# A post-norm decoder layer on one core: earlier first projections, two waits moved, another order of all steps

## The chip, the cores and the metric

The kernel runs on one core of one Trainium2 chip. The metric is device time in microseconds (us), the median of three runs; smaller is better. Inside the core, TensorE (PE) multiplies matrices, VectorE (DVE) and ScalarE (ACT) work on the results in PSUM and SBUF, GpSimd (POOL) does a few masks and sums, and DMAs are issued from the queues of SyncE (SP), ACT and POOL.

## What is computed

One transformer layer over x and ctx of shape (16, 128, 128), float32: self-attention with relative positions, causal cross-attention with ctx, and a feed-forward part with eight routed experts and a shared one. After each of the three, the residual is added and the sum normalised.

```python
# self-attention: E = 128, H = 16 heads of 8, relative positions clipped at 20
attn = softmax((q @ k.T + q @ rk2.T) / sqrt(8))
x = layernorm(x + ((attn @ v + attn @ rv2) @ Wo.T + bo))
# cross-attention, causal: queries from x, keys and values from ctx
x = layernorm(x + softmax(mask(cq @ ck.T / sqrt(8))) @ cv @ cWo.T + cbo)
# feed-forward: probs = softmax(x @ router_w + router_b), the best 2 of 8 experts, one shared expert
x = layernorm(x + gelu(x @ sw1 + sb1) @ sw2 + sb2
                + sum_e weight_e * (gelu(x @ rw1[e] + rb1[e]) @ rw2[e] + rb2[e]))
```

## The kernel before

The 16 sequences are worked in four chunks of four (512 tokens). All work of a chunk is cut into named steps, and one string, `SCHEDULE` (lines 74 to 102), lists the steps of all chunks in one order: the digit ahead is the chunk, a number behind a dot the tile. Every engine's program, and SP's queue, walks this same list (`for s in ORDER`) and executes its own part of each step. Inside an engine nothing overtakes, so a step that waits holds back all that stands behind it on that engine. The string is written out by hand or by a planner outside the kernel; no time is worked out at run time.

The steps of a chunk, in the order of their data:

- `load`, `loadc`: SP loads x (four DMAs, L340) and ctx (one DMA, L345). Chunk 0's are issued ahead of the list, `load` of chunk 1 at its place in it. A load of x for chunk 2 or later waits for the residual sum of two chunks before.
- `xT`: PE transposes x (L515), ACT copies it (L761). `q`, `k`, `v`: the projections (PE L520 for q and k, L526 for v). Each of q, k, ck and cq is split into three bf16 parts: ACT writes the high part (L789), DVE the rest (L922), ACT the middle (L791), DVE the low part (L926). Then SP writes the parts to DRAM (`parts_by_head<-part`, L389) and, in the step `st_q`, `st_k`, `st_ck` or `st_cq`, waits for that write and reads them back stacked by head into QS or KS with three DMAs (L404). `v` and `cv` end in a DVE add of the value bias (L933).
- `bias` (8 tiles, PE L636, ACT copy L799): relative-position scores. It needs stacked q.
- `p1` (8 tiles, PE L547): scores, which DVE adds (L943) and reduces to maxima (L946). It needs stacked k. `m` (twice): PE transposes the maxima, DVE splits them in three (L958 to L969), ACT and SP send them into rows of QS (L775, L412). `p2` (8 tiles, PE L556) takes the maxima off; DVE adds (L974), ACT takes the exponential (L803).
- `pv`, `w2`, `pvT`, `w2T` (4 each): values, relative values and transposes back. `X`, `XT`, `o`, `ln`: divide, project, add the residual, normalise. `x1T`, `cq` start the cross-attention.
- `cT`, `ck`, `cv`; `c1` (8 tiles, maxima by DVE L950), `cm`, `c2` (8 tiles, exponential L810), `cpv`, `cpvT`, `cX`, `cXT`, `co`, `cln`: cross-attention, which needs `st_ck` and `st_cq`.
- `x2T`, `r`, `g`, `up` (18 matmul steps, PE L714, GELU on ACT L846), `dn` (9, PE L725, DVE L1060), `fln` (last normalisation on DVE, L886 to L896, and the store of the output from SP, L432).
- `wts`: the weights of cross-attention are transposed (PE L507). `lrv`: relative values by way of DRAM. `lex`: ten DMAs on SP (L371 to L384) load all expert weights and biases.

PE has two large PSUM slots for `bias`, `p1`, `p2`, `c1`, `c2` and four small ones for the rest; each use waits until the slot's last user has been read.

Around the change: PE executes `wts` and `xT` first and, behind the first `xT`, the transposes of the self-attention weights and of the bias columns (L598). Then `q`, `k` and `v` of chunk 0 wait (L609 and L610) for `wt_sb` to reach 3. ACT counts `wt_sb` up once for the weights of q and k (L744), once for those of v and o (L746) and once for the bias columns (L766). The fourth use of a small slot waits in addition for a DVE memset of that bank (L878). DVE waits at L879 for all four value and output biases before it begins the list. The first `ADD` that reads them is the one of `v`.

Of the kernel before, what the change touches and what calls it, by code (L numbers as in the profile page):

```python
# [80 lines left out]
0cpv.1 0c2.5 0c2.6 1m.1 2q 0c2.7 2st_q 1pv.0 0cpv.2 0cpvT.0 1p2.2 0cpvT.1 1p2.3 1pvT.0 1p2.4 0cpv.3 0cpvT.2  # L81
1p2.5 1pv.1 1p2.6 0cpvT.3 1p2.7 0cX 1cv 1pv.2 1ck 1w2.0 0cXT 2k 1pvT.1 1w2.1 1w2.2 1pv.3 0co 1w2.3 1pvT.2 1pvT.3
2bias.0 2bias.1 0cln 1st_ck 1w2T.0 1w2T.1 1w2T.2 2bias.2 1w2T.3 0x2T 2bias.3 1X 2bias.4 0r 1XT 2v 2bias.5 0up.0
1o 2bias.6 0up.1 0g 1ln 2bias.7 0up.2 2p1.0 0dn.0 1x1T 2st_k 2p1.1 2cT 1cq 0up.3 2p1.2 2p1.3 0up.4 1st_cq 0up.5
0dn.1 0up.6 3load 0up.7 2p1.4 2p1.5 0up.8 0dn.2 1c1.0 0up.9 0up.10 2m.0 3xT 1c1.1 1c1.2 0dn.3 1c1.3 1c1.4 0up.11
1c1.5 1cm.0 0up.12 0up.13 2p2.0 0dn.4 2p2.1 1c1.6 0dn.5 1c2.0 1c2.1 0dn.6 1c1.7 1c2.2 2ck 1cpv.0 1c2.3 2pv.0
2p2.2 1cm.1 1cpvT.0 0up.14 2p1.6 0up.15 0up.16 0up.17 2p2.3 2p1.7 1cpv.1 0dn.7 1c2.4 1c2.5 2m.1 3q 0dn.8 1c2.6
1c2.7 1cpv.2 2pv.1 2p2.4 2pvT.0 1cpvT.1 2p2.5 1cpvT.2 2p2.6 1cpv.3 2p2.7 2cv 2pvT.1 2pv.2 1cpvT.3 2w2.0 2pvT.2
# [1010 lines left out]
```

## Time and profile before

| | us |
|---|---|
| median of three runs | 451.35 (451.09 to 451.75) |
| profiled execution | 451.89 |
| its span, first to last instruction | 450.1 |
| PE busy in the span | 378.3 |
| DVE busy | 303.4 |
| ACT busy | 228.3 |
| POOL busy | 80.0 |

The profile is of one execution, on which the trace gives each instruction's start and duration. PE busy counts matmuls with modelled ends. "issue" names time in which an engine waited for nothing that the profile shows. A row of SPq, ACTq or POOLq is the issuing of DMAs, not their transfer.

### The profile page before, as it was taken

Reading aid. Unit: us, or ns where it says so; the run is one execution under the profiler, and the core shown is the slowest. Engines: PE = TensorE matmul, PEld = TensorE weight load, DVE = VectorE, ACT = ScalarE, POOL = GpSimd, SP = SyncE. Lnnn points to the kernel's source line nnn. Section 1 sums busy time; section 2 is a strip of 40 time slices with the busy share of each in tenths; the row PEclk is TensorE's granted clock in tenths of the full one; section 3 lists DMA queues with packets and bytes.
Section 4 is the critical chain, followed back from the end, with each engine's and each line's share of the span. In section 5 each row is a group of like instructions: output and inputs, shape, how many; then the busy total and the mean of one; then the engine's idle time right before and its main releaser. Section 6 shows DMA issues by size and latency. Waiting matters only on the chain.

```text
span 450.1 us, 11284 instructions
## 1 busy us (share of the span) xinstructions
PE 378.3 (84%) x4714; PEld 285.1 (63%) x4729; DVE 303.4 (67%) x630; ACT 228.3 (51%) x329; POOL 80.0 (18%) x92
## 2 busy tenths in 40 slices
...
GB/s 93 73 183 39 4 51 248 202 71 128 28 4 41 108 178 1 128 4 4 39 39 82 214 4 106 4 37 4 75 3 2 100 31 6 1 1 0 25 1 23
DMA packets 29420, 26.87 MB, mean 60 GB/s; under 512 B 12673, under 2 KB 27962, under 8 KB 28602
## 3 DMA queue, kind: packets, MB, share of 16 engines
...
q8 instruction: 38, 0.62, 0.6%
q10 hardware_dynamic: 3136, 0.27, 0.5%
q14 instruction: 12, 0.10, 0.1%
q0 software_dynamic: 192, 0.03, 0.0%
...
## 4 chain that ended last, share of the span: by engine, by line
PE 54%; DVE 17%; DMA 10%; issue 6%; ACT 5%; SPq 5%; POOL 1%; POOLq 0%; DVEq 0%; ACTq 0%
PE ps_f L725 9%; PE ps_s L547 9%; PE ps_f L714 8%; PE ps_f L573 6%; PE ps_f L581 4%; DMA parts_by_head<-part 3%; PE ps_f L677 3%; PE ps_f L520 3%; DMA QS<-parts_by_head 3%; DVE ST L943 3%; PE ps_s L540 3%; DVE MX L946 3%; PE ps_s L556 2%; PE ps_f L526 2%; PE ps_s L636 2%
## 5 line engine op out<-in xcount | busy, mean ns | idle before, releaser
L547 PE MATMUL ps_s<-QS,KS 125*128 125x128 bf16 (+1 forms) x768 | 79.5, 249 | 11.9 <-DVE ST L943 6.6
L547 PEld LDWEIGHTS ps_s<-QS,KS 125*128 125x128 bf16 (+1 forms) x768 | 65.1, 106 | 34.6 <-DVE ST L943 9.0
L846 ACT ACTIVATE HT<-ps_f,hb 128x512 f32<-128x512 f32 x72 | 48.3, 688 | 74.0 <-PE ps_f L714 44.3
L725 PEld LDWEIGHTS ps_f<-w,HT 128*128 128x128 f32 x576 | 68.8, 192 | 8.1 <-issue 6.0
L725 PE MATMUL ps_f<-w,HT 128*128 128x128 f32 x576 | 72.1, 276 | 0.1
L714 PE MATMUL ps_f<-x2T,w 128*128 128x512 f32 x144 | 70.8, 602 | 1.4 <-DVE acc L1056 1.0
L488 POOL TENSOR_SCALAR_AFFINE_SELECT PC<-PC 128x1024 f32<-128x1024 f32 x32 | 34.8, 1094 | 142.2 <-ACT PC L810 142.2
L1060 DVE SCALAR_TENSOR_TENSOR acc<-ps_f,gw,acc 128x128 f32<-128x128 f32 x128 | 35.7, 341 | 21.8 <-PE ps_f L725 21.5
L810 ACT ACTIVATE PC<-ps_s 128x1024 f32<-128x1024 f32 x32 | 32.2, 1024 | 33.4 <-PE ps_s L547 30.1
L803 ACT ACTIVATE ST<-ST 128x1024 f32<-128x1024 f32 x32 | 33.9, 1061 | 28.0 <-DVE ST L974 27.6
L943 DVE TENSOR_TENSOR ST<-ps_s,ST 128x1024 f32<-128x1024 f32 x32 | 38.6, 1207 | 11.0 <-PE ps_s L547 10.9
L974 DVE TENSOR_TENSOR ST<-ps_s,ST 128x1024 f32<-128x1024 f32 x32 | 38.2, 1216 | 8.6 <-PE ps_s L556 8.2
L950 DVE TRANSPOSE_TENSOR_REDUCE MX<-ps_s 128x32 f32<-128x1024 f32 x32 | 38.7, 1232 | 3.8 <-PE ps_s L547 3.6
L946 DVE TRANSPOSE_TENSOR_REDUCE MX<-ST 128x32 f32<-128x1024 f32 x32 | 39.8, 1245 | 1.1
L494 POOL TENSOR_TENSOR ve<-mv,epst 128x4 f32<-128x4 f32 x12 | 2.4, 202 | 197.1 <-DVE mv L890 197.1
L714 PEld LDWEIGHTS ps_f<-x2T,w 128*128 128x128 f32 x144 | 24.1, 191 | 16.3 <-issue 13.9
L799 ACT COPY ST<-ps_s 128x1024 f32<-128x1024 f32 x32 | 30.9, 1025 | 6.9 <-PE ps_s L636 6.9
L540 PE MATMUL ps_s<-maskT,identb 128*128 128x512 bf16 x64 | 25.8, 402 | 8.7 <-DMA QS<-parts_by_head 5.8
L922 DVE SCALAR_TENSOR_TENSOR rest<-ps_f,bcol,part 128x512 f32<-128x512 f32 x16 | 11.9, 743 | 22.0 <-ACT part L789 22.0
L636 PE MATMUL ps_s<-QS,RK 125*128 125x64 bf16 x512 | 20.5, 197 | 5.9 <-issue 3.7
L636 PEld LDWEIGHTS ps_s<-QS,RK 125*128 125x128 bf16 x512 | 18.9, 101 | 7.9 <-issue 4.4
L556 PE MATMUL ps_s<-QS,onesr 128*128 128x512 bf16 x49 | 17.4, 422 | 6.9 <-DMA QS<-MP 4.3
...
## 6 DMA issues: line engine op xcount, KB each, us to landing
...
QS<-MP SPq DMA_DIRECT2D x32, 8.0 KB, 2.1
```

Source lines behind the costliest of these rows:

```text
L488: nc.gpsimd.affine_select(out=w, in_=w, compare_op=ALU.is_ge, fill=0.0, base=0, pattern=[[0, HB_TILE], [1, S]], channel_multiplier=-1).the ...
L540: nc.tensor.matmul(ps[:, half * BANK:(half + 1) * BANK], identb[:, :], maskT[:, :, :].broadcast_to([P, 4, S]), start=True, stop=False, ski ...
L547: last = nc.tensor.matmul(ps[:, o:o + S], KS[a][0:kd, c:c + S], queries(a, kd, h, j), start=not masked and j == 0, stop=j == NB - 1, skip_ ...
L636: last = nc.tensor.matmul(ps[:, j * HB:(j + 1) * HB], RK[0:KZ, S - 1 - q:2 * S - 1 - q], qs_q[:, :, q, :], start=True, stop=True)
L714: nc.tensor.matmul(ps[:, :], w1[:, e, f * P:(f + 1) * P], x2T[:, :], start=True, stop=True).then_inc(f_full, 1)
L725: last = nc.tensor.matmul(ps[:, b * E:(b + 1) * E], HT[n % 2][:, f, b * S:(b + 1) * S], w2[:, e, f, :], start=f == 0, stop=f == NF - 1 and ...
L846: nc.scalar.activation(HT[n % 2][:, f, :], ps[:, :], ACT.Gelu, bias=hb[:, e, f:f + 1]).then_inc(ht_ready, 1)
L943: nc.vector.tensor_tensor(by_bank(w), ps[:, :].rearrange("p (c b q) -> p c q b", b=2, q=S), by_bank(w), ALU.add).then_inc(sum_ready, 1)
L946: nc.vector.tensor_reduce(MX[0][:, t * 32:(t + 1) * 32], w.rearrange("p c (g i) -> p c g i", i=QD), AXIS.X, ALU.max, apply_transpose=True) ...
L950: nc.vector.tensor_reduce(MX[1][:, t * 32:(t + 1) * 32], ps[:, :].rearrange("p (c i) -> p c i", i=QD), AXIS.X, ALU.max, apply_transpose=Tr ...
L974: nc.vector.tensor_tensor(w, ps[:, :].rearrange("p (c i) -> p c i", i=ST_PAIR), w, ALU.add).then_inc(sc_ready, 1)
L1060: last = nc.vector.scalar_tensor_tensor(acc[:, b, :], ps[:, b * E:(b + 1) * E], gw[ch % 2][:, b, t - 1:t], acc[:, b, :], ALU.mult, ALU.add)
```

## The change

Three edits. `q` and `k` of chunk 0 wait for the first weight copy alone, `v` for the second. DVE's wait for the value biases moves from ahead of the list to the first `v` and the first `cv`. And `SCHEDULE` is replaced by another order of the same steps.

```diff
                     if ch == 0:
-                        pe.wait_ge(wt_sb, 3)
+                        pe.wait_ge(wt_sb, 2 if what == "v" else 1)
...
             nc.vector.memset(ps_f[3][:, :], 0.0).then_inc(c_dve, 1)
-            v.wait_ge(ld_br, 16 * 4)
...
                     if ch:
                         done_f(v, (ch - 1, "cpv" if a else "pv", NQ - 1))
+                    else:
+                        v.wait_ge(ld_br, 16 * 4)
```

The order, cut to its head and to the places of which the prediction speaks:

```diff
-0xT 1xT 0load 1load 0loadc 0q 0st_q 0k 0v 0st_k 0wts 0cT 0ck 0cv 0bias.0 0bias.1 0bias.2 0bias.3 0bias.4 0bias.5
-0bias.6 0bias.7 0p1.0 0p1.1 0p1.2 0p1.3 0p1.4 0m.0 0p1.5 0lrv 0p1.6 0p2.0 0p1.7 0p2.1 0m.1 0p2.2 0pv.0 0p2.3
-0p2.4 0lex 0pvT.0 0p2.5 0pv.1 0p2.6 0p2.7 1q 1st_q 0pv.2 0w2.0 0w2.1 0pvT.1 0pvT.2 0st_ck 0pv.3 1k 0w2.2 0w2.3
-1v 0pvT.3 0w2T.0 0w2T.1 0w2T.2 0w2T.3 1bias.0 1bias.1 0XT 1bias.2 1loadc 0X 1bias.3 0o 1bias.4 0ln 1st_k 1bias.5
-1bias.6 1bias.7 1p1.0 0x1T 1cT 0cq 1p1.1 1p1.2 1p1.3 1p1.4 0st_cq 2loadc 0c1.0 0c1.1 0c1.2 0c1.3 1m.0 0c1.4
-2load 0cm.0 0c1.5 0c1.6 0c1.7 1p1.5 0c2.0 0c2.1 0c2.2 0cm.1 1p2.0 1p1.6 0cpv.0 0c2.3 2xT 1p2.1 1p1.7 0c2.4
+0load 0xT 1load 0q 0k 0v 1xT 0wts 0bias.0 0bias.1 0bias.2 0bias.3 0bias.4 0st_q 0bias.5 0bias.6 0st_k 0bias.7
+0p1.0 0loadc 0p1.1 0p1.2 0p1.3 0lrv 0p1.4 0m.0 0p1.5 0cT 0p1.6 0p2.0 0p1.7 0p2.1 0m.1 0p2.2 0pv.0 0p2.3 0p2.4
+0p2.5 0pv.1 0p2.6 0pvT.0 0p2.7 1q 0pv.2 1st_q 0ck 0w2.0 0w2.1 0w2.2 0st_ck 1k 0pvT.1 1st_k 0pv.3 0w2.3 0pvT.2
+0pvT.3 0w2T.0 0w2T.1 0w2T.2 0w2T.3 1bias.0 1bias.1 0lex 0X 1v 0XT 1bias.2 1bias.3 0o 1bias.4 1bias.5 1loadc
+1bias.6 0ln 0cv 1bias.7 1p1.0 0x1T 0cq 2load 1p1.1 1p1.2 1p1.3 1p1.4 0st_cq 2xT 0c1.0 1cT 0c1.1 0c1.2 0c1.3
+0c1.4 0cm.0 0c1.5 0c1.6 0c1.7 0c2.0 0c2.1 1m.0 0c2.2 0cm.1 1p1.5 0c2.3 0cpv.0 1p2.0 1p2.1 1p1.6 0cpv.1 0c2.4
...
-3w2T.1 3w2T.2 3w2T.3 2x2T 3X 3cv 2r 3XT 2up.0 3o 1dn.8 2up.1 2up.2 2g 2up.3 3ln 1fln 3x1T 3cq 2up.4 2dn.0 2up.5
-2up.6 2dn.1 2up.7 2dn.2 2dn.3 3c1.0 3c1.1 2up.8 3st_cq 3c1.2 3c1.3 3c1.4 2up.9 3cm.0 3c1.5 2up.10 3c1.6 2up.11
-3c1.7 3c2.0 2dn.4 3c2.1 3cm.1 2dn.5 3c2.2 3c2.3 3cpv.0 3c2.4 3c2.5 3cX 3cpv.1 3c2.6 3c2.7 3cpvT.0 3cpv.2 3cpvT.1
-2up.12 3cpvT.2 3cpv.3 2up.13 3cpvT.3 2dn.6 3cXT 2up.14 3co 2up.15 3cln 2up.16 2dn.7 2up.17 3x2T 3r 3up.0 3up.1
+3pv.0 3p2.4 2cXT 3p2.5 3pv.1 3p2.6 3p2.7 2co 3pvT.0 1dn.8 2cln 3w2.0 3w2.1 1fln 3pvT.1 3pv.2 2x2T 3pv.3 2r 2up.0
+3w2.2 3w2.3 3pvT.2 3pvT.3 3w2T.0 3w2T.1 3w2T.2 3w2T.3 3X 2up.1 2g 3cv 3XT 2up.2 3o 2dn.0 2up.3 2up.4 3x1T 2up.5
+3ln 3cq 2up.6 2dn.1 2up.7 2dn.2 2up.8 2up.9 2dn.3 2dn.4 3c1.0 3c1.1 3c1.2 3c1.3 3st_cq 3c1.4 2up.10 3cm.0 3c1.5
+2up.11 3c1.6 2up.12 3c1.7 3c2.0 3c2.1 3cm.1 2dn.5 3c2.2 3c2.3 3cX 3cpv.0 3c2.4 3c2.5 3cpvT.0 3cpv.1 3c2.6 3c2.7
+3cpv.2 3cpvT.1 2up.13 3cpv.3 3cpvT.2 3cpvT.3 2dn.6 3cXT 2up.14 3co 2up.15 2up.16 3cln 2dn.7 2up.17 3x2T 3r 3up.0
...
```

## Rows read from the trace of the kernel before

**Rows 1.** Stretches: us, busy by engine, PEclk granted clock, DMA share, GB/s.

```profile
core 0: us, PE busy (x) PEld busy (x) DVE busy (x) ACT busy (x) POOL busy (x), PEclk, DMA share, GB/s
0.00:29.00 29.00, 10.48 (x46) 6.98 (x46) 13.02 (x22) 8.08 (x15) 23.04 (x30) 1.00 0.41 109
29.00:60.00 31.00, 16.63 (x198) 12.86 (x199) 21.52 (x23) 8.58 (x9) 0.00 (x0) 0.61 0.19 56
...
100.00:125.00 25.00, 14.49 (x114) 9.56 (x113) 22.70 (x29) 0.62 (x1) 0.00 (x0) 0.78 0.26 70
125.00:300.00 175.00, 172.09 (x2296) 133.59 (x2304) 142.71 (x285) 110.91 (x161) 28.42 (x30) 0.99 0.22 62
300.00:412.00 112.00, 103.60 (x1283) 76.45 (x1285) 68.51 (x182) 66.00 (x95) 23.60 (x25) 1.00 0.10 26
```

**Rows 2.** Timeline, opening, PE and DVE: start, duration, what, [idle before <- releaser].

```profile
8.06 0.27 PE L598 MATMUL ps_f<-ident,OW 4*128 4x4 f32 x1 [1.04 <-DMA OW<-in_L_xattn_bk]
...
10.46 0.48 DVE L878 MEMSET ps_f<- 128x512 f32 x1
...
14.95 1.11 PE L515 MATMUL ps_f<-ident,xin 128*128 128x128 f32 x4 [6.63 <-DMA xin<-in_x]
```

**Rows 3.** The chain that ended last, single pieces: start, duration, what.

```profile
10.41 4.50 DMA xin<-in_x
...
91.41 3.69 DMA KS<-parts_by_head
...
101.49 2.52 DMA parts_by_head<-part
...
105.22 4.26 DMA QS<-parts_by_head
...
122.53 2.00 DMA QS<-MP
...
281.93 1.84 PE ps_f L725 x16
...
292.23 1.77 PE ps_f L714 x4
```

**Rows 4.** Timeline, opening: the query parts from the high part to the first bias.

```profile
17.81 0.69 ACT L789 ACTIVATE part<-ps_f,bcol 128x512 bf16<-128x512 f32 x1 [1.06 <-PE ps_f L520]
...
20.79 0.39 SPq L389 DMA_DIRECT2D parts_by_head<-part  x1
...
23.41 1.83 SPq L404 DMA_DIRECT2D QS<-parts_by_head  x3
...
28.92 1.87 PE L636 MATMUL ps_s<-QS,RK 125*128 125x64 bf16 x32 [3.67 <-issue]
```

**Rows 5.** Timeline, opening: the key parts and the first scores.

```profile
25.29 0.58 SPq L389 DMA_DIRECT2D parts_by_head<-part  x1
...
29.89 1.74 SPq L404 DMA_DIRECT2D KS<-parts_by_head  x3
...
36.93 2.02 PE L547 MATMUL ps_s<-QS,KS 125*128 125x128 bf16 x16 [0.36 <-ACT ST L799]
```

**Rows 6.** Timeline of SP's queue, first and last expert load, chunk 1's q stack, x of chunk 2.

```profile
63.02 0.58 SPq L371 DMA_DIRECT2D rb_row<-in_L_ffn_router_b  x1
...
72.25 0.53 SPq L384 DMA_DIRECT2D wr<-in_L_ffn_router_w  x1
...
78.06 2.14 SPq L404 DMA_DIRECT2D QS<-parts_by_head  x3
...
119.47 2.08 SPq L340 DMA_DIRECT2D xin<-in_x  x4
```

**Rows 7.** Stretches again: the one in which the expert weights arrive.

```profile
66.00:76.00 10.00, 6.72 (x185) 4.19 (x185) 6.03 (x6) 8.00 (x11) 0.00 (x0) 0.98 0.86 239
```

**Rows 8.** Timeline, DVE and PE, chunk 3 ahead of its cross-attention.

```profile
350.32 2.06 DVE L896 TENSOR_SCALAR acc<-acc,mv,rstd 128x128 f32<-128x128 f32 x4 [1.40 <-POOL rstd L496]
...
363.15 0.38 PE L540 MATMUL ps_s<-maskT,identb 128*128 128x512 bf16 x1 [1.45 <-DMA QS<-parts_by_head]
```

More of the change, by code:

```diff
@@ L80 @@
-2load 0cm.0 0c1.5 0c1.6 0c1.7 1p1.5 0c2.0 0c2.1 0c2.2 0cm.1 1p2.0 1p1.6 0cpv.0 0c2.3 2xT 1p2.1 1p1.7 0c2.4
[L81 to L88, printed above, removed]
-2w2.1 3st_q 1cX 0fln 1cXT 2w2.2 3k 2pv.3 1co 3st_k 2w2.3 3bias.0 3bias.1 2pvT.3 3v 2w2T.0 3loadc 2st_ck 1cln
@@ L100 @@
-3up.2 2dn.8 3up.3 3g 3up.4 2fln 3up.5 3dn.0 3up.6 3dn.1 3dn.2 3up.7 3up.8 3up.9 3dn.3 3up.10 3up.11 3up.12 3dn.4
-3dn.5 3up.13 3up.14 3up.15 3up.16 3up.17 3dn.6 3dn.7 3dn.8 3fln
+0load 0xT 1load 0q 0k 0v 1xT 0wts 0bias.0 0bias.1 0bias.2 0bias.3 0bias.4 0st_q 0bias.5 0bias.6 0st_k 0bias.7
+0p1.0 0loadc 0p1.1 0p1.2 0p1.3 0lrv 0p1.4 0m.0 0p1.5 0cT 0p1.6 0p2.0 0p1.7 0p2.1 0m.1 0p2.2 0pv.0 0p2.3 0p2.4
+0p2.5 0pv.1 0p2.6 0pvT.0 0p2.7 1q 0pv.2 1st_q 0ck 0w2.0 0w2.1 0w2.2 0st_ck 1k 0pvT.1 1st_k 0pv.3 0w2.3 0pvT.2
@@ new lines @@
+0pvT.3 0w2T.0 0w2T.1 0w2T.2 0w2T.3 1bias.0 1bias.1 0lex 0X 1v 0XT 1bias.2 1bias.3 0o 1bias.4 1bias.5 1loadc
+1bias.6 0ln 0cv 1bias.7 1p1.0 0x1T 0cq 2load 1p1.1 1p1.2 1p1.3 1p1.4 0st_cq 2xT 0c1.0 1cT 0c1.1 0c1.2 0c1.3
+0c1.4 0cm.0 0c1.5 0c1.6 0c1.7 0c2.0 0c2.1 1m.0 0c2.2 0cm.1 1p1.5 0c2.3 0cpv.0 1p2.0 1p2.1 1p1.6 0cpv.1 0c2.4
+1p1.7 0c2.5 2q 0cpvT.0 0c2.6 0c2.7 1m.1 0cpv.2 0cpvT.1 2loadc 1pv.0 1p2.2 1p2.3 1cv 0cpv.3 1p2.4 0cpvT.2 1p2.5
+1pv.1 1p2.6 1pvT.0 1p2.7 0cpvT.3 1pv.2 0cX 1pvT.1 1ck 1w2.0 1pv.3 2st_q 2k 1pvT.2 1w2.1 2v 0cXT 1w2.2 0co 1w2.3
```

20 lines of the change are left out of this document (14 added, 6 removed).

## The prediction, written before the changed kernel ran

> **What bounds the kernel now.** I read the stretches first [rows 1]. From 125 to 300 us PE is busy 172.1 of 175.0 us, so there the time is PE's own work, and no order shortens that. Ahead of it PE lacks 18.5 us of the first 29, 14.4 of the next 31 and 10.5 of the 25 us from 100. Behind it, from 300 to 412, it lacks 8.4. The same steps are executed after the change, so the time falls by what these gaps lose, and rises by new ones. The reader should see there that a gain in the opening is kept if nothing later is tied to a fixed moment, because the saturated stretch simply starts earlier.
>
> Then the timeline of the opening [rows 2]. PE ends the bias columns at 8.33 and next works at 14.95, on the transpose of chunk 1's x, which stands ahead of 0q in the list. That x is issued last of all first loads and lands at 14.91 by the chain of waits [rows 3]. Nothing that chunk 0 needs is missing: q waits behind a step of another chunk.
>
> **The first edit** (wait for one weight copy). In PE's own order q stands behind the bias columns, whose matmul ends at 8.33 [rows 2]; the third count follows by one small ACT copy, about 0.2 us. The edit is worth 0.2 at most, and I count it within the next term.
>
> **1xT behind 0v.** q's matmuls start at 8.4. In the trace they took from 16.06 (14.95 + 1.11 [rows 2]) to the high part at 17.81 [rows 4], 1.75, so the high part starts at 10.1, ends at about 10.8, and DVE is free at 10.94, behind its memset [rows 2]. From high part to the write of the parts the trace has 20.79 - 17.81 = 2.98 [rows 4]: 13.2 with a tenth of waiting, 7.6 earlier than 20.79. The write landed in 2.62 (23.41 - 20.79, [rows 4]); k's, which shared the DMA engines with a stack, in 4.60 (29.89 - 25.29, [rows 5]). The new write shares its first 1.7 us with the end of x, so I take 3.3, nearer the first. From the stack's issue to the first bias the trace has 28.92 - 23.41 = 5.5 [rows 4]. First bias: 13.2 + 3.3 + 5.5 = 22.0, or **6.9 earlier**. With 2.62 it is 7.6; with 4.6, and 0.5 for k's write now ahead of the stack, 5.1. Below zero is excluded, since every step of that chain moves forward.
>
> Keys: k's parts are ready about 2.3 behind q's, 15.5; they land by 20.1, and st_k, behind st_q on SP, has its data by 20.1 + 1.2 + 3.7 = 25.0 (the 3.7 from [rows 3]). The eight bias tiles need 8.0 us (36.93 - 28.92, [rows 4, 5]), to 30.0. Keys are no bound, and the phase that follows, where DVE sets the pace (21.5 busy of 31 us [rows 1]), begins 6.9 earlier as a whole.
>
> **The second edit** (value biases). In the old order DVE's first piece of the list followed the high part that starts at 17.81 [rows 4], long after any bias, so the wait cost nothing. In the new order it would hold q's rest from 11.0 until the biases are there; they are issued just ahead of x, so by 14.9 at the latest [rows 3]. The edit is worth 0 to 3.9 in the new order, and is what lets the term above stand.
>
> **0cT, 0ck, 0cv out of the opening.** They hid in the wait for q's stack, so leaving it earns nothing. 0cT (about 0.6 of PE) now hides in PE's gaps of the p1 phase. 0ck comes between 1q and 0w2.0, and its write and stack stand on SP ahead of 1k's write. Queue: 1q's write as before, stack, ck's write, stack of ck, k's write, stack of k, each stack (1.8 of issuing, [rows 4, 5]) waiting for a landing of 2.5 to 4.6 [rows 3, 5]. From the issue of 1st_q to the landed keys that is 1.8 + 2.5 + 1.8 + 2.5 + 1.2 + 3.7 = 13.5, or 17.7 with both landings long, against 17.0 in the trace (91.41 + 3.69 - 78.06, [rows 3, 6]). PE reaches 1bias somewhat earlier, an estimated 1.6, as 1v moved behind its first tiles, and then waits for these keys. Ends: 1.6 gained, 0.7 lost; I take **0.3 gained**.
>
> **Expert loads (lex) later.** Before, they were issued from 63.02 to 72.78 [rows 6], and the engines were 0.86 busy at 239 GB/s from 66 to 76 [rows 7]; nobody waited. Now the same 9.8 us of issuing stand between 1st_k and the write of 0cq's parts. 1st_k ends about when 1p1.0 becomes possible less 3.7, and cq's parts are ready 10 us after it (101.49 against 91.4 [rows 3]), so the queue is free within a microsecond either way. But their transfers are still running, and x of chunk 2 (2.08 of issuing [rows 6]) now stands behind cq's write too. So I give that write 4.6, the longest of [rows 5], instead of 2.52 [rows 3]. The data of c1.0 then come 2.1 later than their 109.48; DVE has its p1 tiles in hand at that time and sets the pace there [rows 1], so I let more than half of it hide. **0.8 lost**; ends 0 and 3.5, the latter with 1.5 more from the two DMAs that follow. The Trainium skill ("DMA: Bandwidth & Descriptors", "Queues, rings and completion order") says that each of the 16 DMA engines takes one issuer's descriptors in ring order; this is the rule that speaks against the change. By it the write of cq's parts lies behind all that is left of the experts, the 3.5 end; no row here shows such a meeting.
>
> **Cross-attention of chunk 0.** In the trace SP had x of chunk 2 (2.08) ahead of the second shift, which landed at 124.53 [rows 3, 6], and c2.0 waited for it. Now x is issued long before, and 1m.0 and 1p1.5 (some 3.6 of DVE, 1.3 of PE) come behind c2.0, so c2.0 comes about 2.0 earlier. PE owes 0.7 of that later (2xT, 0.6, is already done), and DVE, 22.7 busy of 25 [rows 1], owes all 3.6, part of which shows. **0.5 gained**; ends -1.5 and +1.3.
>
> **The middle.** 125 to 300 has 2.9 us of gaps in 175 [rows 1]. The fillers between cq and c1.0 of chunk 2 fall by one `up` (0.9, half of 1.77 for two [rows 3]), so **0.5 lost**, ends -1.5 and +1.
>
> **Chunk 3.** In the trace 1fln stands ahead of 3cq's parts on DVE: it holds DVE until 352.4 [rows 8], some 1.5 past the high part, and PE then lacks 1.45 at 363.15 [rows 8]. The new order puts 1fln some twenty steps ahead: **1.4 gained**. But two `up` and one `dn` (2 x 0.9 + 1.8 = 3.7, [rows 3]) are gone from the fillers of 3c1 to 3cXT, where DVE and ACT set the pace. Some of the 8.4 us of gaps [rows 1] lie there already, and fewer fillers bring the shifts sooner, so I charge **0.5**; ends 0 and 2. From 3x2T on PE's order is the same but for two groups of `up` and `dn`, and each gelu still ends under a `dn`: zero.
>
> **Sum:** -6.9 - 0.3 + 0.8 - 0.5 + 0.5 - 1.4 + 0.5 = -7.3. The profiled execution took 451.89, its span 450.1 and 1.8 around it, and lies 0.5 above the median; on the median, 451.35 - 7.3 = **444.0**. The sums of the ends are about +3 and -14, but they would have to fall together.
>
> **The rivals.**
> 1. More is gained: the landings take the short values (7.6 instead of 6.9, ck's 1.6 instead of 0.3, experts 0 instead of 0.8, c2.0 1.3, fillers 0 instead of 1.0 in both places): -7.6 - 1.6 - 1.3 - 1.4 = -11.9, 439.5. For it: 2.5 is the commonest landing where engines are free. Against: SP stacks ck between them.
> 2. The experts' transfers delay cq's parts by 3.5, and the stack of q in the opening takes its long value: -7.3 + 2.7 + 1.0 = -3.6, 447.7. For it: 0.86 busy for 10 us [rows 7].
> 3. Same: the earlier opening is given back in full, as it would be if some later step hung on a fixed moment. I find no such step; each load is issued well ahead.
> 4. Slower, 453: the place is the write of 0cq's parts behind the experts. By ring order each later DMA of SP (x of chunk 2, the stack of cq) queues there too. They decide once c1.0 comes over 7.3 + 1.3 = 8.6 later on its own scale; the expert loads took some 13 us from issue to silence (63 to 76), so if 1st_k and they start together and all three DMAs of the chain wait, the price is 9 to 10. Against: the queue issues in order, and nearly 10 us pass before cq's write is issued.
> 5. The edit of the waits does nothing by itself (0.2); that is already in the sum.
>
> **How the numbers follow.** Forecast 0.55, with its own range 442 to 446.5; rival 1 0.20; rival 2 0.15; rival 3 0.03; rival 4 0.07. A measurement of this kernel tells about 0.2%, 0.9 us, from no change. Faster 0.90 (forecast and rivals 1 and 2), same 0.03, slower 0.07. The range leaves out rivals 3 and 4 and the far part of 1: 439.0 to 448.6.
>
> **What would show it.** Right: PE L520 at 8.4, the first query write at 13.2, the first L636 at 22, the first L547 at 30; the same distance from 3x2T to the end. c1.0 of chunk 0 near 103; PE over 98% busy from there plus 15; no wait of 1.45 ahead of 3c1.0. Wrong: a first bias later than 24, a write of cq's parts that lands over 5 us after its issue, or gaps over 5 us in what was the saturated stretch.

## The result, and the profile after

The changed kernel took 455.94 us (454.19 to 458.64, 4 runs) beside 451.22 (450.95 to 451.75, 4 runs) of the kernel before on the same chip: ratio 1.0119, interval [1.0073, 1.0164]. It is slower by 1.2%, where 1.6% faster (444.0) was predicted. The profiled execution took 456.95, its span 455.2.

Read the same points of both traces first; the distance between neighbouring rows says where time came or went.

| start, us | before | after | difference |
|---|---|---|---|
| first bias tile (first L636) | 28.92 | 22.31 | -6.6 |
| first scores of chunk 0 (first L547) | 36.93 | 30.94 | -6.0 |
| first scores of chunk 1, 1p1.0 | 95.15 | 94.10 | -1.1 |
| first cross-attention scores, 0c1.0 (first L540) | 109.72 | 112.27 | +2.6 |
| first router matmul (L702) | 164.44 | 167.43 | +3.0 |
| last router group | 404.24 | 408.95 | +4.7 |
| end of span | 450.1 | 455.2 | +5.1 |

So the opening did what was forecast and its gain was gone at the first chunk-1 scores. From 31 to 112 us the changed kernel loses 8.5 us, and later 2.5 more.

The stretches of the kernel after, same columns as [rows 1]:

```profile
0.00:29.00 29.00, 14.81 (x131) 11.10 (x132) 9.23 (x19) 11.44 (x18) 23.02 (x30) 0.79 0.60 155
29.00:60.00 31.00, 17.25 (x140) 11.30 (x139) 25.55 (x31) 6.72 (x8) 0.00 (x0) 0.56 0.02 3
60.00:100.00 40.00, 31.10 (x579) 22.92 (x580) 18.70 (x34) 22.50 (x33) 2.51 (x3) 0.84 0.47 123
100.00:125.00 25.00, 14.36 (x111) 9.57 (x108) 20.10 (x23) 1.79 (x3) 1.26 (x1) 0.68 0.41 113
125.00:300.00 175.00, 168.02 (x2281) 129.90 (x2289) 142.84 (x285) 111.69 (x159) 27.12 (x29) 1.00 0.23 63
```

PE works 4.3 us more in the first 29. DVE, the pace-setter of the next stretch, works 4.0 more. From 100 to 125 it falls back to 20.10, and "saturated" 125 to 300 now has gaps of 7.0 us, not 2.9.

The timeline of PE and of SP's queue in the opening answers to [rows 2] and [rows 4]:

```profile
8.10 3.78 PE L520 MATMUL ps_f<-TR,wT 128*128 128x512 f32 x4
...
22.31 1.87 PE L636 MATMUL ps_s<-QS,RK 125*128 125x64 bf16 x32 [6.37 <-DMA QS<-parts_by_head]
...
30.94 2.02 PE L547 MATMUL ps_s<-QS,KS 125*128 125x128 bf16 x16 [0.28 <-ACT ST L799]
```

```profile
13.23 2.47 SPq L389 DMA_DIRECT2D parts_by_head<-part  x2
15.94 1.85 SPq L404 DMA_DIRECT2D QS<-parts_by_head  x3
```

Projections at 8.10, the first write at 13.23, landed by 15.94 (2.7), the first bias at 22.31: each within 0.6 of the forecast.

Now SP's queue around the two steps that moved, after:

```profile
70.60 0.37 SPq L389 DMA_DIRECT2D parts_by_head<-part  x1
74.75 2.50 SPq L404 DMA_DIRECT2D QS<-parts_by_head  x3
77.30 0.58 SPq L389 DMA_DIRECT2D parts_by_head<-part  x1
81.62 2.65 SPq L404 DMA_DIRECT2D KS<-parts_by_head  x3
84.31 0.58 SPq L389 DMA_DIRECT2D parts_by_head<-part  x1
88.48 1.74 SPq L404 DMA_DIRECT2D KS<-parts_by_head  x3
90.27 0.58 SPq L371 DMA_DIRECT2D rb_row<-in_L_ffn_router_b  x1
...
100.69 0.47 SPq L384 DMA_DIRECT2D wr<-in_L_ffn_router_w  x1
...
101.81 0.42 SPq L389 DMA_DIRECT2D parts_by_head<-part  x1
102.27 2.20 SPq L340 DMA_DIRECT2D xin<-in_x  x4
106.75 1.79 SPq L404 DMA_DIRECT2D QS<-parts_by_head  x3
```

Three round trips through DRAM stand one behind the other: 1's queries at 70.60, 0's cross keys at 77.30, 1's keys at 84.31. Before, the cross keys had been written long ago, and only their stack stood between. Then ten expert loads take the queue from 90.27 to 101.16, and the write of 0cq's parts follows at 101.81, with the load of ctx between them. Before, the first query write of chunk 1 and the stack of cq stood here:

```profile
75.53 0.37 SPq L389 DMA_DIRECT2D parts_by_head<-part  x1
...
104.07 1.74 SPq L404 DMA_DIRECT2D QS<-parts_by_head  x3
```

The chain of waits, after, says what each landing took (start, duration):

```profile
70.60 4.14 DMA parts_by_head<-part
...
77.30 4.26 DMA parts_by_head<-part
...
84.31 4.15 DMA parts_by_head<-part
...
89.63 4.42 DMA KS<-parts_by_head
...
101.81 4.88 DMA parts_by_head<-part
...
107.95 4.04 DMA QS<-parts_by_head
```

From the first write to landed keys that is 94.05 - 70.60 = 23.5 us; before it was 95.10 - 75.53 = 19.6 ([rows 3] and the write above). And the write of cq's parts took 4.88 where [rows 3] have 2.52. PE, after, shows the waits for the keys and for cq's stack, and a third thing:

```profile
94.10 1.09 PE L547 MATMUL ps_s<-QS,KS 125*128 125x128 bf16 x8 [4.96 <-DMA KS<-parts_by_head]
...
96.72 2.08 PE L520 MATMUL ps_f<-TR,wT 128*128 128x512 f32 x2 [0.68 <-ACT TR L761]
...
112.27 0.58 PE L540 MATMUL ps_s<-maskT,identb 128*128 128x512 bf16 x1 [3.49 <-DMA QS<-parts_by_head]
```

The same cq projection took 1.12 before (at 97.36) and 2.08 now. The stretch around it, before and then after, says why: the granted clock.

```profile
90.00:102.00 12.00, 8.56 (x114) 6.97 (x110) 7.51 (x18) 7.84 (x10) 2.52 (x3) 1.00 0.21 67
```

```profile
90.00:102.00 12.00, 5.85 (x30) 3.96 (x30) 4.82 (x7) 2.08 (x4) 1.26 (x1) 0.59 0.83 212
```

The mean granted clock of these 12 us, of which PE idled 5 for the keys, is 0.59 instead of 1.00, and from 94 to 107 it is 0.50, the lower of the two levels (1.2 GHz). So one late landing is paid twice, once as a wait, and once in the matmuls behind it.

The 8.5 us can be laid out along this chain. The first `pv` (first L573) starts at 61.84 before and at 55.85 now, so the whole gain of 6.0 is still there. 1.1 is lost by the write of 1's query parts (75.53 and 70.60), 3.9 more by the keys, and 3.6 between 1p1.0 and 0c1.0: 1.4 ahead of cq's write, 1.0 of it in the slower projection, 2.4 in the landing of that write (106.75 - 101.81 against 104.07 - 101.49), and nothing behind it.

### The profile page after: what moved, and what is told of

Its sections match the earlier page's. It is cut to its first block, busy times and chain, and to the rows that moved or that the text cites. A ratio compares the mean times of both kernels' runs of the same rounds, so it can differ in the third digit from the quotient of the medians.

```text
span 455.2 us, 11291 instructions
## 1 busy us (share of the span) xinstructions
PE 382.0 (84%) x4716; PEld 286.2 (63%) x4729; DVE 303.6 (67%) x630; ACT 231.4 (51%) x331; POOL 79.9 (18%) x92
## 4 chain that ended last, share of the span: by engine, by line
PE 53%; DVE 18%; DMA 14%; ACT 5%; issue 4%; SPq 3%; POOL 1%; ACTq 1%; POOLq 0%; DVEq 0%
PE ps_f L714 10%; PE ps_f L725 8%; PE ps_s L547 8%; DMA parts_by_head<-part 6%; PE ps_f L573 5%; PE ps_f L581 4%; DMA QS<-parts_by_head 4%; DVE ST L944 3%; DVE MX L947 3%; PE ps_s L540 3%; PE ps_s L556 2%; DVE MX L951 2%; PE ps_s L636 2%; PE ps_f L520 2%; PE ps_f L677 2%
## 5 line engine op out<-in xcount | busy, mean ns | idle before, releaser
L547 PE MATMUL ps_s<-QS,KS 125*128 125x128 bf16 (+1 forms) x768 | 78.2, 245 | 16.7 <-DVE ST L944 6.6
L547 PEld LDWEIGHTS ps_s<-QS,KS 125*128 125x128 bf16 (+1 forms) x768 | 63.5, 105 | 41.1 <-issue 10.1
L714 PE MATMUL ps_f<-x2T,w 128*128 128x512 f32 x144 | 71.8, 601 | 1.3 <-DVE acc L1057 1.3
L803 ACT ACTIVATE ST<-ST 128x1024 f32<-128x1024 f32 x32 | 33.6, 1058 | 17.7 <-DVE ST L975 17.1
L810 ACT ACTIVATE PC<-ps_s 128x1024 f32<-128x1024 f32 x32 | 32.5, 1028 | 19.3 <-PE ps_s L547 14.2
L799 ACT COPY ST<-ps_s 128x1024 f32<-128x1024 f32 x32 | 31.2, 1019 | 14.9 <-PE ps_s L636 14.8
L540 PE MATMUL ps_s<-maskT,identb 128*128 128x512 bf16 x64 | 25.4, 396 | 8.3 <-DMA QS<-parts_by_head 5.6
L636 PE MATMUL ps_s<-QS,RK 125*128 125x64 bf16 x512 | 22.2, 204 | 10.7 <-DMA QS<-parts_by_head 6.4
L636 PEld LDWEIGHTS ps_s<-QS,RK 125*128 125x128 bf16 x512 | 20.5, 105 | 13.7 <-issue 11.2
L556 PE MATMUL ps_s<-QS,onesr 128*128 128x512 bf16 x51 | 18.5, 439 | 8.4 <-DMA QS<-MP 4.7
L581 PE MATMUL ps_f<-ident,OT 128*128 128x128 f32 x128 | 20.0, 284 | 1.3 <-ACT OT L818 1.3
```

Source lines behind the costliest of these rows:

```text
L540: nc.tensor.matmul(ps[:, half * BANK:(half + 1) * BANK], identb[:, :], maskT[:, :, :].broadcast_to([P, 4, S]), start=True, stop=False, ski ...
L547: last = nc.tensor.matmul(ps[:, o:o + S], KS[a][0:kd, c:c + S], queries(a, kd, h, j), start=not masked and j == 0, stop=j == NB - 1, skip_ ...
L581: last = nc.tensor.transpose(ps[:, j * P:(j + 1) * P], src(j), ident[:, :])
L636: last = nc.tensor.matmul(ps[:, j * HB:(j + 1) * HB], RK[0:KZ, S - 1 - q:2 * S - 1 - q], qs_q[:, :, q, :], start=True, stop=True)
L714: nc.tensor.matmul(ps[:, :], w1[:, e, f * P:(f + 1) * P], x2T[:, :], start=True, stop=True).then_inc(f_full, 1)
```

## The experiments

Medians have their lowest and highest run behind them; ratios are to the kernel before on the same chip, whose medians were 450.86 to 451.27. "Head" is the list up to 0c1.0. Single milestones come from one profiled execution each, which is the fastest run of e1, e2, e8, e12, e13 and e14 and the slowest of e4 and x3.

**The waits alone, and the opening alone.** e1 has the old order with both edited waits:

```diff
-pe.wait_ge(wt_sb, 3)
+pe.wait_ge(wt_sb, 2 if what == "v" else 1)
...
-v.wait_ge(ld_br, 16 * 4)
```

> The old order with both wait edits alone. Theory A (the opening gain is real and the new order spends it between 60 and 112 us, by three round trips of projection parts through DRAM one behind another on SP's queue, and by the expert loads ahead of cq's parts) gives no part of it to the waits: in the old order q stands behind chunk 1's x, so 451.2 within 0.9. Theory B (the waits themselves cost something, as an earlier DVE or PE step now collides with POOL or a DMA) expects 452.5 or more.

Measured 451.03 (450.1 to 451.86), 0.9999 [0.9977, 1.0022]. The waits do nothing in the old order. e2 has the waits and, of the new order, 1xT's place alone:

```diff
-0xT 1xT 0load 1load 0loadc 0q 0st_q 0k 0v 0st_k 0wts
+0load 0xT 1load 0loadc 0q 0st_q 0k 0v 1xT 0st_k 0wts
```

> The old order, with both wait edits and one move: 1xT and 1load's neighbours so that q, k and v of chunk 0 stand ahead of 1xT; all other steps in their old places, ck and the expert loads too. Theory A: the first bias tile at 22.3 us as in the changed kernel, and 5 to 6.5 us of it kept to the end, so 445 to 446.5. Theory C (an earlier opening is always given back, as PE and the DMA landings after it are worse off whatever the order): 449.5 to 452.

Measured 444.72 (443.67 to 445.32), 0.9864 [0.9815, 0.9913]. First bias at 21.65, 1p1.0 at 88.03, 0c1.0 at 102.84, last router group at 396.4: 6.7 to 7.8 earlier all the way. What the opening gains is kept by everything behind it, so the rest of the change costs 11.2.

**Undoing ck and the experts in the changed kernel.** e3 puts the expert loads back:

```diff
-1bias.1 0lex 0X
+1bias.1 0X
...
-0p2.4 0p2.5
+0p2.4 0lex 0p2.5
```

> The changed kernel with lex back behind 0p2.4. Theory A: the write of cq's parts (issued 101.81, landed 4.88 later) lands in about 2.6, and st_cq and c1.0 come 2.3 to 3 earlier, near 109.5; to the end 453 to 454 against 455.9. Theory C: no gain that lasts, 455 to 457.

Measured 450.79 (446.95 to 453.04), 0.9979 [0.9943, 1.0015]: 5.15 gained. 0c1.0 stood at 108.55, its write landed in 2.8, but PE still waited 5.85 for chunk 1's keys. e4 moves only ck into the opening:

```diff
-0wts 0bias.0
+0wts 0cT 0ck 0bias.0
...
-0p1.5 0cT 0p1.6
+0p1.5 0p1.6
...
-1st_q 0ck 0w2.0
+1st_q 0w2.0
```

> The changed kernel with 0cT and 0ck back between 0wts and 0bias.0; lex and all else as changed. Theory A: SP no longer waits for ck's landing (4.3 us, 77.30 to 81.56) between 1st_q and the write of 1k's parts, 1k comes earlier on PE too, and 1p1.0 comes at 89.5 to 91 in place of 94.10, then bound by the bias tiles; 452 to 453.5 at the end. Theory C: 455 to 457.

Measured 457.45 (455.66 to 458.17), 1.0143 [1.009, 1.0196]: no better, and for a reason of its own. In this order ck's write stands ahead of the stack of queries on SP. The queue, e4:

```profile
13.41 8.17 SPq L388 DMA_DIRECT2D parts_by_head<-part  x3
21.70 1.84 SPq L403 DMA_DIRECT2D QS<-parts_by_head  x3
```

All later work began 5.7 late, so the time of e4 says nothing on ck itself, though PE's wait for 1's keys fell to 2.18. It shows a rule of this kernel: a write waits on SP for its parts, and whatever is behind it waits too. e5 puts both back, with the stacks ahead:

```diff
-0wts 0bias.0 0bias.1 0bias.2 0bias.3 0bias.4 0st_q 0bias.5 0bias.6 0st_k 0bias.7
+0wts 0st_q 0st_k 0cT 0ck 0bias.0 0bias.1 0bias.2 0bias.3 0bias.4 0bias.5 0bias.6 0bias.7
...
-0p1.5 0cT 0p1.6
+0p1.5 0p1.6
...
-1st_q 0ck 0w2.0
+1st_q 0w2.0
...
-0p2.4 0p2.5
+0p2.4 0lex 0p2.5
...
-1bias.1 0lex 0X
+1bias.1 0X
```

> The changed kernel with lex back behind 0p2.4, and 0cT and 0ck before the bias tiles, this time behind 0st_q and 0st_k, so that SP doesn't wait for ck's parts ahead of the stacks. Theory A (DRAM round trips in a row and experts): first bias at 22.3, 1p1.0 at 87.5 to 89 (94.10 as changed), c1.0 at 103 to 104.5 (112.27), 444.5 to 447 at the end. Theory D (what follows c1.0 in the new order costs 2 to 3 us more than in the old): 447 to 449 with the same c1.0.

Measured 445.56 (444.42 to 447.03), 0.987 [0.9834, 0.9906]. Only 0.8 over e2: nearly all of the loss hangs on these two steps, and the rest of the new order is worth little either way. (The two stacks moved with them, but q's stack was issued at 16.03 in e15, which has the same opening, and at 15.94 in the changed kernel.) PE of e5 no longer waits for keys, nor loses its clock:

```profile
87.30 1.09 PE L546 MATMUL ps_s<-QS,KS 125*128 125x128 bf16 x8
...
89.68 1.13 PE L519 MATMUL ps_f<-TR,wT 128*128 128x512 f32 x2 [0.68 <-ACT TR L760]
```

**The same two moves, made in the old order.** e7 is e2 with the experts late:

```diff
-0p2.4 0lex 0pvT.0
+0p2.4 0pvT.0
...
-1st_k 1bias.5
+1st_k 0lex 1bias.5
```

> The old order with the opening moved (444.72) and lex alone moved behind 1st_k, as in the new order. Theory A: the write of cq's parts is issued near 94.7 to 95.5 and lands 4.5 to 5 later in place of 2.55, c1.0 2.5 to 3.5 later than 102.84, and 447 to 448.5 at the end. If the experts are harmless without the other moves: 444 to 445.5.

Measured 446.44 (443.2 to 446.96), 0.9866 [0.9815, 0.9917]: 1.7 over e2. cq's write needed 4.56, and 0c1.0 came 17.75 us behind 1p1.0 where e2 has 14.8. Part of this lies ahead of the write, which was issued 7.7 behind 1p1.0 (6.6 in e2): cq's projection ran at half clock (2.08), and the queue was 0.5 late with the loads. 1p1.0 itself came 1.3 earlier than in e2. e8 is e2 with ck late:

```diff
-0cT 0ck 0cv
+0cT 0cv
...
-0pv.2 0w2.0
+0pv.2 0ck 0w2.0
```

> The old order with the opening moved (444.72) and 0ck alone moved behind 0pv.2, as in the new order. Theory A: the write of ck's parts and its landing (4.3) stand on SP between 1st_q and the write of 1k's parts; 1p1.0 at 91 to 93 in place of 88.03, and 447.5 to 449.5 at the end. If the landing hides behind the bias tiles of chunk 1: 444 to 446.

Measured 445.96 (444.88 to 446.95), 0.9877 [0.9845, 0.9909]: 1.2 over e2. Both together, e11 (the two diffs above):

> The old order with the new opening (e2, 444.72) and both moves together: 0ck behind 0pv.2 (alone 445.96, +1.2) and the expert loads behind 1st_k (alone 446.44, +1.7). If their costs just add: 447.7, c1.0 of chunk 0 near 105.6. If they collide (ck delays the keys, so the expert loads start later and lie more on cq's parts, and PE waits and loses its clock): 449.5 to 451, c1.0 at 107 or later. If the one hides in the other: 446.4.

Measured 450.38 (448.51 to 453.0), 0.9982 [0.9959, 1.0004]: 5.7 over e2, twice the sum of the single costs. PE of e11 waits 5.43 for the keys; e7 waited 1.53 and e8 1.23. So nearly the whole gain of the opening can be lost by these two moves.

**Where ck costs.** e9 is e3 with ck behind 1's keys on SP:

```diff
-1st_q 0ck 0w2.0 0w2.1 0w2.2 0st_ck 1k 0pvT.1 1st_k 0pv.3
+1st_q 0w2.0 0w2.1 0w2.2 1k 0ck 0pvT.1 1st_k 0st_ck 0pv.3
```

> The changed kernel with two things put back or moved: the expert loads early, as in e3, and the step 0ck with its stack not ahead of chunk 1's keys but behind them (1k 0ck 1st_k 0st_ck), so that SP writes and stacks 1's keys first. Theory (what costs 1p1.0 six us in the changed kernel is ck's round trip standing on SP between the query stack and the key write of chunk 1): first chunk-1 score near 88 us instead of 92.8 in e3, c1.0 of chunk 0 at 103 to 105, median 446 to 447.5, against e3's 450.79. Rival (the new order has its 1q later and its p2 and pv steps at a slow TensorE clock, and the ck trip is only along for it): first chunk-1 score at 91 or later, median 449.5 or more. If ck's own stack is now what c1.0 waits for, the first holds at 1p1.0 and the median stays above 448.

Measured 448.38 (448.05 to 449.87), 0.9946 [0.9926, 0.9967]: 2.4 better than e3, 2.8 short of e5, between the two theories. PE of e9 did not wait for keys at 1p1.0, and still came to it only 0.6 before e3 (92.80), and 4.9 behind e5 (87.30). By this milestone the rival (91 or later) was right:

```profile
92.21 0.97 PE L546 MATMUL ps_s<-QS,KS 125*128 125x128 bf16 x7
```

The round trip between queries and keys is thus only one part of the price: without it there is no wait of 5.85, cq's projection keeps its clock (1.12, not 2.08), and 0c1.0 comes 1.5 earlier than in e3. Another part is ck's work itself, which stands between 1k and the transposes of the relative values: from 76 to 81 us DVE has two pairs of rest and low part (0.75 and 0.69) where e2 has one, and PE waits 1.08 for a rest. A third part is the clock behind these waits: the 16 transposes of `w2T` took 3.43 at a granted clock of 0.55 (80.8 to 84.1), in e5 1.91 at 1.00.

**Where the experts cost.** e13 is e2 with the experts behind cq's stack, neither early nor ahead of it:

```diff
-0p2.4 0lex 0pvT.0
+0p2.4 0pvT.0
...
-0st_cq 2loadc
+0st_cq 0lex 2loadc
```

> The old order with the new opening (e2, 444.72), the expert loads behind the stack of 0cq (0st_cq) instead of behind 0p2.4. Two theories are priced at once. Collision: with the experts issued behind cq's write and stack nobody on SP's chain waits for them, so c1.0 comes 14 to 15 us behind the first chunk-1 score as in e2 (14.8), not 17.8 as in e7. Hole: the idle 2.4 us that PE shows inside the w2 matmuls, without any releaser, stands only in runs whose expert weights arrive at that time (before, e1, e2, e5, e9, e10, e12), so it should be gone here and the first chunk-1 score come at 86.7 as in e7, not 88.0. Both right: c1.0 near 101.5, median 443.3 to 444.0. Rival: the experts, issued from 98 to 108, delay the maxima of cross-attention or x of chunk 2 instead, and the hole only moves: median 445 to 447.

Measured 443.66 (441.65 to 445.62), 0.9845 [0.9819, 0.9872], the fastest median of all, though its runs overlap with those of e2. 0c1.0 came 15.0 behind 1p1.0, as the collision theory has it. Of the 2.75 by which that is shorter than in e7, 2.0 are the landing (2.58 against 4.56); 1.4 lie ahead of the write, where cq's projection kept its clock, and 0.6 goes the other way behind it. The stretch in which the write of cq's parts lands, DMA view of e13 and then of e7 (share of the DMA engines in 40 slices, and GB/s):

```profile
DMA  0000000000000269999999999899996200000000
GB/s 0 0 0 0 0 0 0 0 0 0 0 0 0 76 228 394 334 379 319 349 349 379 319 394 334 288 379 319 394 334 198 61 0 0 0 0 0 0 0 0
```

```profile
DMA  9999999999999999998875553221111000000000
GB/s 296 279 314 296 248 270 283 266 262 303 261 301 300 344 312 342 346 393 272 283 253 180 175 183 109 85 70 52 44 44 52 26 26 17 17 0 0 0 0 0
```

In e13 the engines are silent, take the write at some 290 to 390 GB/s and are done: 2.5 us. In e7 they are busy from the first slice on, where the write can't have started yet (in e13 its data begin 0.9 us behind the issue): 0.86 MB pass in that window, 0.39 in e13, and it takes 4.6. e14 is the changed kernel with that same move of the experts:

```diff
-1bias.1 0lex 0X
+1bias.1 0X
...
-0st_cq 2xT
+0st_cq 0lex 2xT
```

> The changed kernel (455.94) with the one move of e13: expert loads behind 0st_cq. If what the experts cost in the changed kernel is only that cq's write and stack queue behind them: c1.0 at 94.1 plus 15, 109, 3 us earlier, and the median 452.5 to 453. If they also cost elsewhere in the new order (e3, with the experts early, gained 5.15): 450.8. If experts at this place hit chunk 2's x and the maxima: 455 or more.

Measured 453.0 (449.46 to 455.5), 1.0044 [1.0016, 1.0073]: 2.9 better than the changed kernel, 16.3 between 1p1.0 and 0c1.0 instead of 18.2. The runs scatter by 6 us, so this size is rough, and beside e16 (below: the changed kernel's order with the old waits, 453.81) it is 0.8. Whether this move helps in the new order is therefore not shown. e15 closes the square in the new order, e5 with the experts late:

```diff
-0p2.4 0lex 0p2.5
+0p2.4 0p2.5
...
-1bias.1 0X
+1bias.1 0lex 0X
```

> Completes a square in the new order: e5 has both 0ck in the opening and the experts early (445.56), e3 only the experts early (450.79), the changed kernel neither (455.94). This one is e5 with the expert loads where the changed kernel has them. If their costs add, 445.56 + 5.15 = 450.7. If they need each other, as the same square in the old order says (444.72, 445.96, 446.44, both 450.38): 447 to 448, with keys on time (no wait over 2 us ahead of the first chunk-1 score) and c1.0 17.8 behind it.

Measured 449.57 (446.86 to 451.69), 0.9967 [0.9944, 0.999]. The two squares:

| median, us | neither late | ck late | experts late | both late |
|---|---|---|---|---|
| old order, new opening | 444.72 | 445.96 | 446.44 | 450.38 |
| new order | 445.56 | 450.79 | 449.57 | 455.94 |

In the new order the costs are 5.2 and 4.0, and 10.4 together, nearly a sum; the guess that they need each other holds for the old order alone. The corner of 455.94 has 4 runs. e16, which has the same order and 12 runs, makes it 453.81, and both together 8.3.

Why the experts cost more there (4.0 against 1.7) lies only in small part behind 1p1.0. x of chunk 2 now stands between cq's write and its stack, and its transpose ahead of 0c1.0 on PE, and e15 waited at both places:

```profile
102.86 1.11 PE L514 MATMUL ps_f<-ident,xin 128*128 128x128 f32 x4 [2.34 <-DMA xin<-in_x]
107.70 0.58 PE L539 MATMUL ps_s<-maskT,identb 128*128 128x512 bf16 x1 [3.73 <-DMA QS<-parts_by_head]
```

But the wait for QS is the one that ends last, and 0c1.0 stood 18.45 behind 1p1.0, 0.7 more than in e7, with a landing of 5.2 instead of 4.6 and the queue 1.0 late instead of 0.5. The larger part lies ahead: 1p1.0 came 2.0 later in e15 (89.25) than in e5, while in e7 it came 1.3 earlier than in e2.

**A clock that rises late.** What delays 1p1.0 in e15 can be seen ahead of 1q. The changed kernel and e16 have the same list; their first `pv` starts at 55.85 and 57.08, and 1q at:

```profile
65.21 1.02 PE L520 MATMUL ps_f<-TR,wT 128*128 128x512 f32 x2
```

```profile
64.74 1.02 PE L520 MATMUL ps_f<-TR,wT 128*128 128x512 f32 x2
```

From the first `pv` to 1q it is 9.3 to 9.4 us in the changed kernel, e3, e4 and e15, and 7.7 in e5, e9, e14 and e16 (7.2 to 7.5 in the old order). Between 4.0 and 7.2 us behind the first `pv` the granted clock was 0.50 in the first four, and 0.82 to 1.00 in the second four. The changed kernel and e16 differ by the two waits alone. So 1.7 us in the profiles of the changed kernel, e3 and e15, which e5's has not, need not be a price of the two moves. Whether the medians of these kernels differ by it too, and what lets the clock rise sooner, no run shows.

**The later part.** x3 is e2's head with the rest of the list in the new order:

```diff
-0st_cq 2loadc 0c1.0 0c1.1 0c1.2 0c1.3 1m.0 0c1.4 2load 0cm.0
+0st_cq 2loadc 2load 2xT 0c1.0 0c1.1 0c1.2 0c1.3 0c1.4 0cm.0
...
```

> The old order with the opening moved up to 0c1.0 of chunk 0, and from there all remaining steps in the new order. Theory A: the new rest is worth about nothing by itself, 444 to 446, with 1fln ahead of 3cq gone and 3c1.0 less late. Theory D: the new rest costs 2 to 3, 446.5 to 448.

Measured 446.38 (446.03 to 447.83), 0.9893 [0.9861, 0.9924]. Its 0c1.0 stood 17.8 behind 1p1.0, since the join put 2load and 2xT between 0st_cq and 0c1.0 and PE waited 5.88 for x there. That is an artefact of the cut, and the 1.7 over e2 includes it, so what the new rest costs by itself is not shown but should be less. e10 tries the prediction's term for chunk 3 in the old order:

```diff
-3pvT.2 2cln 3pvT.3 3w2T.0 3w2T.1 3w2T.2 3w2T.3 2x2T
+3pvT.2 1dn.8 2cln 3pvT.3 3w2T.0 3w2T.1 3w2T.2 3w2T.3 1fln 2x2T
...
-3o 1dn.8 2up.1 2up.2 2g 2up.3 3ln 1fln 3x1T
+3o 2up.1 2up.2 2g 2up.3 3ln 3x1T
```

> The old order with the new opening (e2, 444.72) and one more thing from the new order: 1dn.8 ahead of 2cln and 1fln ahead of 2x2T, where the old order has both just ahead of 3's cross-attention. The prediction gave the wait of 1.45 ahead of 3c1.0 to 1fln on DVE and took 1.4 for it: median 443.3, and no wait over 0.5 ahead of 3c1.0. Rival: PE is near its own limit there and the wait only moves (to DVE's next piece, or to the stack of 3cq): median 444.4 to 445.2.

Measured 449.69 (447.08 to 451.08), 0.9956 [0.9935, 0.9977]: 5.0 slower than e2. PE of e10:

```profile
336.91 1.11 PE L514 MATMUL ps_f<-ident,Y 128*128 128x128 f32 x4 [3.04 <-DVE Y L990]
```

1fln on DVE now stands ahead of 3X, and PE waits for Y. The place is not quite that of the new order, where more of 3's pv and w2 stands behind 1fln. So e10 shows that the step can cost, not what it did in the changed kernel.

**The waits inside the new opening.** e12 is e2 with both old waits, e16 the changed kernel's order with both old waits (the diff of e1, reversed).

> The old order with the new opening (e2, 444.72), but with both waits as in the kernel before: so the order alone. The four bias loads land near 12.4 us (7.95 plus 4.4), and DVE began the first rest of q at 11.23 in e2, so the waits should cost 1.1 on the first query write (13.4 becomes 14.5) and 0.2 for the third weight count is hidden in it: first bias tile near 22.8, median 445.0 to 446.0. Rival: keys and the write's landing swallow it, nothing at 1p1.0, median 444.7. The prediction had 0 to 3.9 for this edit in the new order.

> The changed kernel's order with both waits as in the kernel before. The prediction had 0 to 3.9 for the value biases and 0.2 for the weight count in the new order. In the old order with the new opening the waits cost 1.2 at the first bias tile and 0.9 in the median (e12 445.64 against e2 444.72). If it is the same here: first bias near 23.5, median 456.5 to 457. Rival: later waits swallow it, 456.

e12: 445.64 (443.65 to 446.89), 0.9876 [0.9851, 0.9901], first bias at 22.88 instead of 21.65. The waits bring 1.2 at the first tile, and 0.9 in the median, which the spread of the runs does not prove. e16: 453.81 (451.35 to 459.66), 1.0067 [1.0042, 1.0091], first bias at 23.55. It is 2.1 faster than the changed kernel though its first tile comes 1.2 later, and the two intervals overlap. So nothing of the waits is seen at the end in the new order, and medians of this order are known to some 2 us only. The profile of e16 also shows what the ten loads can do to the queue itself:

```profile
95.93 6.60 SPq L383 DMA_DIRECT2D w<-in_L_ffn_sw  x1
...
103.56 0.51 SPq L389 DMA_DIRECT2D parts_by_head<-part  x1
```

One load took 6.60 to issue, 2.72 in the changed kernel. cq's parts were ready at 100.5, and their write stood 3.0 behind the loads on the queue; 0c1.0 came 21.1 behind 1p1.0. That wait was 2.5 in e4, 1.0 in e15, 0.5 in e7 and nothing in the changed kernel. Why one issue takes so long is open.

## Why the prediction was wrong, point by point

**1xT behind 0v, -6.9: right.** 6.6 in the changed kernel, 7.3 in e2, kept to the end (e2). Two misses offset each other in it: the write landed 0.6 sooner than taken, and from the stack's issue to the first bias it was 6.4 (22.31 - 15.94), not 5.5. (Rival 2 took 1.0 for the long value of this term; by the prediction's own ends, 6.9 and 5.1, it is 1.8.) The bias tiles took 8.6 and not 8.0, since PE met them after 6.4 us of idling: its granted clock was 0.51 from 22 to 31, where the tiles of before had 0.79 (29 to 37).

**The waits: right.** Both together brought nothing in the old order (e1) and 0.9 in the new opening (e12), within the spread of the runs, inside the 0 to 3.9 and at its low end. The first edit was not run alone.

**ck out of the opening, -0.3 (1.6 gained to 0.7 lost): this step failed.** Measured: 1.2 lost in the old order (e8), 5.2 in the new (e3 against e5), of which 1.7 may be the late clock of e3's profile. From the issue of 1st_q's stack to landed keys it came to 94.05 - 74.75 = 19.3; the prediction had 13.5, or 17.7 with both landings long. Even the far end was too near: both landings were long (4.3 and 4.2), the stacks took 2.5 and 2.65 to issue, not 1.8, and the last read 4.42, not 3.7. The write ahead of all this, counted "as before", landed in 4.14 instead of 2.53. And the step priced the queue alone: ck also has 1.44 us on DVE (0.75 and 0.69) and 1.31 on ACT (0.69 and 0.62). PE waits for them, 0.68 in the changed kernel (at 72.35) and 1.08 in e9. That "PE reaches 1bias somewhat earlier" then only makes the wait for keys longer.

**Experts later, +0.8 (0 to 3.5): the mechanism was named, the size was not.** Measured 1.7 in the old order alone, 4.4 with ck late, and 4.0 to 5.2 in the new one (3.0 by e16). Landing 4.88 instead of 2.52, as the 4.6 of the prediction had it. What failed is "more than half of it hides" in DVE's pace. In e5, with the data on time, DVE releases 0c1.0 (102.26, 15.0 behind 1p1.0); with the experts late it is the stack's data, 17.75 to 18.45 behind (21.1 in e16), and DVE itself has less in hand, 20.1 busy of 25 where [rows 1] have 22.7. Rival 4 had the right place and got 0.07 because of "nearly 10 us pass before cq's write is issued". Those 10 us are what the issuing of the loads takes. The last goes out at 100.69, the write at 101.81, and in between there was no pause in which the engines could empty. That the queue is free "within a microsecond either way" held in the changed kernel's profile and failed in e16 (3.0) and e4 (2.5). The changed kernel between 94 and 107:

```profile
94.00:107.00 13.00, 8.03 (x46) 5.57 (x46) 9.06 (x9) 1.89 (x3) 1.26 (x1) 0.50 0.93 254
```

The DMA engines are 0.93 busy, at 254 GB/s. The Trainium skill ("DMA: Bandwidth & Descriptors", "Queues, rings and completion order") has each engine take one issuer's descriptors in ring order, which puts the write behind what is left of the experts. The trace agrees for this write, with 4.88 and 4.56 against 2.5 in e13. That the prediction's 3.5 end is close to the 3.6 by which the distance from 1p1.0 to 0c1.0 grew (18.2 against 14.6) is chance: the write's landing has 2.4 of it, 1.4 lie ahead of the write, and the 1.5 that the 3.5 end had for the two DMAs behind it did not come (5.5 from the stack's issue to 0c1.0, before 5.65).

**The two costs as separate terms: failed.** They were summed one by one. In the old order both together cost 5.7, not 2.9. In the profiles the excess lies ahead of 1p1.0: e11 reaches it 3.5 later than e2, where ck alone costs 1.8 and the experts alone gain 1.3. From there to 0c1.0 e11 took 17.8, as e7 did, so it is no harder meeting with the experts. ck's write at 73.22 landed in 6.1 in e11 and in 4.3 in e8, some 15 us before the first expert load of e11. Why is open. What the long waits do bring is the lower clock: cq's projection took 2.07 to 2.08 where PE had waited 1.53 to 5.85 for the keys (e3, e4, e7, e11, e14, e16), and 1.12 to 1.13 where it had waited 0 to 1.23 (e2, e5, e8, e9, e13). The prediction had no term for that.

**Cross-attention of chunk 0, -0.5, and the middle, +0.5.** 0c1.0 to the first router matmul is 55.2 against 54.7 (54.6 in e16): nothing gained. First to last router group is 241.5 against 239.8, against 238.6 in e2. But e16, with the changed kernel's order, has 239.8, so the 1.7 is not a property of the order that a single profile could show.

**Chunk 3, -1.4 and +0.5: failed.** The wait ahead of 3c1.0 was put down to 1fln. Before, it was 1.45 [rows 8]. The changed kernel and then e2, which keeps 1fln where it was:

```profile
369.77 0.38 PE L540 MATMUL ps_s<-maskT,identb 128*128 128x512 bf16 x1 [1.11 <-DMA QS<-parts_by_head]
```

```profile
355.26 0.38 PE L539 MATMUL ps_s<-maskT,identb 128*128 128x512 bf16 x1 [1.12 <-DMA QS<-parts_by_head]
```

The wait is the same with 1fln early or late; it belongs to the stack's round trip. At most 0.3 was there to gain.

**The account.** From 451.2 of before: opening with the waits -6.5 (e2), rest of the new order +0.8 (e5), ck and experts +10.4 (changed kernel against e5; +8.3 by e16), together 455.9. The prediction gave the last line +0.5. Still open is why these two moves cost 2.6 to 4.7 more in the new order than in the old one. What stands behind 1p1.0, x of chunk 2 among it, gives at most 0.7 (e15 against e7). The first query write of chunk 1 is later in the changed kernel (70.60) than in e11 (67.85), and 2.1 of that lies between the first `pv` and 1q (9.4 against 7.2), 1.7 of it at the lower clock (e16 has 7.7), with nothing tried on it.
